# Expert tiles transposed by VectorE in 32x32 blocks, in place of four TensorE transposes per tile

## The reference, cut to what matters

```python
x = x + attention(layernorm(x), ctx, ctx)                    # 16 batches x 256 rows x 256 columns, 16 heads
x = x + moe(layernorm(x), gate_w, gate_b, w1, b1, w2, b2)    # the part that the change touches
x = x + attention2(ctx, layernorm(x), w_q, w_kv, w_out, b_out)
x = x + ffn(layernorm(x), ...)

def moe(x, gate_w, gate_b, w1, b1, w2, b2):     # 4096 rows, 8 experts, each row goes to its best 2
    logits = flat @ gate_w + gate_b
    topv, topi = lax.top_k(logits, 2)
    topw = softmax(topv)
    for each expert e:
        h = gelu(flat @ w1[e] + b1[e])          # 256 -> 1024
        out = h @ w2[e] + b2[e]                 # 1024 -> 256
        acc = acc + out * weight_of_e
```

## Time and profile before

| | |
|---|---|
| median of 3 runs | 1221.36 us |
| lowest and highest | 1218.73 and 1222.63 us |
| span of the profiled execution | 1218.4 us |
| its own time beside the span | not recorded apart; the span lies 2.96 us under the median |
| PE busy in the span | 1129.2 us, 93% |
| PEld busy | 925.1 us, 76% |
| DVE busy | 908.6 us, 75% |
| ACT busy | 743.3 us, 61% |
| POOL busy | 611.8 us, 50% |

### The profile page before, as it was taken

How to read it: one execution, slowest core, us unless ns; L and a number is a source line. 1 busy time by engine, 2 the same in 40 slices (tenths; PEclk the granted TensorE clock), 3 DMA queues, 4 the chain that set the end, 5 groups by cost and what they waited for, 6 DMA issues and landing times. The chain is left out here.

```text
span 1218.4 us, 26789 instructions
## 1 busy us (share of the span) xinstructions
PE 1129.2 (93%) x9622; PEld 925.1 (76%) x9623; DVE 908.6 (75%) x1303; ACT 743.3 (61%) x983; POOL 611.8 (50%) x607
## 2 busy tenths in 40 slices
PE   3899999989899999999999999857999999999997
PEld 2566666679788999999999999745666666668886
DVE  7899999669488888878878777567888888743332
ACT  4687778856445555554555655365877887764442
POOL 3588777344686886722002000788877876002222
PEclk9999999989899999999999999956999999999999
DMA  6577766359936465523132111165656665402221
GB/s 216 202 254 249 268 237 227 132 201 355 325 127 195 142 190 167 174 100 113 43 112 69 34 52 43 55 229 185 216 196 217 208 229 183 155 28 70 69 69 35
DMA packets 121862, 194.19 MB, mean 159 GB/s; under 512 B 12208, under 2 KB 65456, under 8 KB 121648
## 3 DMA queue, kind: packets, MB, share of 16 engines
q1 hardware_dynamic: 105520, 148.57, 35.6%
q0 software_dynamic: 12656, 39.33, 10.3%
q10 hardware_dynamic: 3600, 5.12, 1.2%
HBM read 92.85 MB, written 51.12 MB: 118 GB/s over the span
## 5 line engine op out<-in xcount | busy, mean ns | idle before, releaser
L2389 PE MATMUL y_ps<-e_w,hiddenT_hi 128*128 x624 | 225.3, 403 | 1.9 <-DVE rows L2509 1.9
L2432 ACT ACTIVATE hidden<-hidden 128x1024 f32<-128x1024 f32 x78 | 82.8, 1062 | 190.6 <-DVE hidden L2470 168.1
L2372 PE MATMUL h_ps<-kvT_hi,tile_w_hi 128*128 128x256 f32 x624 | 179.2, 287 | 6.9 <-DVE kvT_lo L2492 6.9
L1673 DVE TENSOR_REDUCE neg_max<-big 128x4 fp32r<-128x1024 f32 x128 | 154.5, 1222 | 36.4 <-PE big L1397 33.8
L2372 PE MATMUL h_ps<-kvT_lo,tile_w_hi 128*128 128x256 f32 x624 | 178.5, 286 | 0.0
L2372 PE MATMUL h_ps<-kvT_hi,tile_w_lo 128*128 128x256 f32 x624 | 178.4, 286 | 0.0
L2390 PE MATMUL y_ps<-e_w,hiddenT_lo 128*128 x624 | 175.2, 281 | 0.0
L736 DVE TENSOR_REDUCE neg_max<-big 128x4 fp32r<-128x1024 f32 x128 | 155.1, 1217 | 23.3 <-PE big L485 22.0
L1567 ACT ACTIVATE probs<-big 128x1024 f32<-128x1024 f32 x128 | 130.7, 1023 | 46.2 <-PE big L1408 44.1
L644 ACT ACTIVATE probs<-big 128x1024 f32<-128x1024 f32 x128 | 130.6, 1022 | 44.3 <-PE big L496 44.2
L2498 DVE TENSOR_TENSOR hiddenT_lo<-hidden,hiddenT_hi 128x1024 fp32r<-128x1024 f32 x78 | 98.7, 1306 | 58.2 <-ACT hiddenT_hi L2443 53.7
(11 more groups left out here) (282 smaller groups left out, 2565.8 us busy)
## 6 DMA issues: line engine op xcount, KB each, us to landing
q_stack<-q_cut SPq DMA_DIRECT2D x96, 256.0 KB, 2.6
k_stack<-k_cut SPq DMA_DIRECT2D x72, 256.0 KB, 2.7
e_w<-in_L_ffn_w POOLq DMA_DIRECT2D x10, 1024.0 KB, 6.9
slots_out<-rows SPq DMA_DIRECT2D x39, 256.0 KB
slots_in<-rows POOLq DMA_DIRECT2D x37, 256.0 KB
slot_x<-slots_in SPq DMA_DIRECT2D x37, 256.0 KB
vals<-in_v_wide SPq DMA_DIRECT2D x16, 512.0 KB, 4.4
vals<-v_wide SPq DMA_DIRECT2D x16, 512.0 KB, 4.0
```

The source lines that it names most:

```text
L1673: nc.vector.tensor_reduce(neg_max[m % 2][:, :, :, g].rearrange("p q a -> p a q").bitcast(F32R), big[bank][:], AX.X, ALU.max, negate=True). ...
L2372: last = nc.tensor.matmul(h_ps[k][:, f % HF, :], w1[w][b.u][:, c, f * P:(f + 1) * P], xT[a][b.u][:, c, :], start=(n == 0), stop=(n == 3 * ...
L2389: nc.tensor.matmul(y_ps[q][:].rearrange("p s d -> p (s d)"), hT[0][o.u][:, f, rows], both, start=(f == 0), stop=False)
L2432: nc.scalar.activation(half(hidden, k), half(hidden, k), ACT.Gelu).then_inc(gelu_done, 1)
```

## The change

The four PE transposes of a tile go, for the 37 tiles that come through `slots_in`. In their place DVE turns the tile with two `transpose` instructions, each over 128x256 elements in blocks of 32x32. Such an instruction only turns within groups of 32 partitions, so the other part of the transposition is done by the load: SP loads a tile in four DMAs (`PARTS`), each of a quarter of the columns (64) of all 256 rows, into 32 partitions. Block i of 32 rows then stands at block i of the free dimension. So that the two halves of the features (`c`) end up as the two chunks of `xT` in the right channel order, the rows in `norm2` (and so in `slots_in`) are stored with the features n and n+128 side by side (`interleaved`), and whoever reads or writes them steps over every second element.

The turned tile lies in SBUF (`turned`, the memory of `ctx_in0`), no longer in PSUM. The first two tiles are still turned by PE.

```diff
+BLOCK = 32
...
+def interleaved(row):
+    return row.rearrange("p (n c) -> p c n", c=KC)
+
+def in_order_of(row):
+    return row.rearrange("p (c n) -> p c n", c=KC)
...
-                    apply(lambda q: y_out[(b - 1) % 2][:, q, :], lambda q: norm2[(b - 1) % 2][:, q, :],
+                    apply(lambda q: in_order_of(y_out[(b - 1) % 2][:, q, :]), lambda q: interleaved(norm2[(b - 1) % 2][:, q, :]),
                           rstdb, mean_varb, rstd2_ready, norm2_ready, b - 1)
...
-                                                   norm2[f % 2][:, q, c * P:(c + 1) * P], ident[:])
+                                                   interleaved(norm2[f % 2][:, q, :])[:, c], ident[:])
...
-                    nc.vector.tensor_scalar(norm2[f % 2][:, q, :], y_out[f % 2][:, q, :], mean_varb[:, q, 0:1], rstdb[:, q:q + 1],
+                    nc.vector.tensor_scalar(interleaved(norm2[f % 2][:, q, :]), in_order_of(y_out[f % 2][:, q, :]), mean_varb[:, q, 0:1], rstdb[:, q:q + 1],
...
         def loaded(n):
-            return n.n * 16
+            return n.n * PARTS * 16
+
+        def in_parts(n, part):
+            rows = dram["slots_in"][bass.ds(n.t * SLOT_ROWS, SLOT_ROWS), part * KC * BLOCK:(part + 1) * KC * BLOCK]
+            return rows.rearrange("(i b) k -> b i k", b=BLOCK)
+
+        def of_part(n, part):
+            return x[n.u][part * BLOCK:(part + 1) * BLOCK].rearrange("b q (i k) -> b (q i) k", k=KC * BLOCK)
...
+        def transposed(n):
+            return xT_ps[:] if n.t0 < EARLY_TILES else turned
...
-                    sp.dma_start(x[n.u][:], tiled(dram["slots_in"], n.t)).then_inc(x_loaded[n.u], 16)
+                    for part in range(PARTS):
+                        sp.dma_start(of_part(n, part), in_parts(n, part)).then_inc(x_loaded[n.u], 16)
...
-                if has(n.t):
+                if has(n.t) and n.t0 < EARLY_TILES:
                     turn_x(n)
...
-                        nc.scalar.activation(xT[0][n.u][:], xT_ps[:], ACT.Copy).then_inc(xT_hi, 1)
+                        nc.scalar.activation(xT[0][n.u][:], transposed(n), ACT.Copy).then_inc(xT_hi, 1)
...
+            def turn_x(n):
+                dve.wait_ge(x_loaded[n.u], loaded(n))
+                dve.wait_ge(xT_ready, n.t)
+                alone(dve)
+                for c in range(KC):
+                    last = nc.vector.transpose(turned[:, c, :].rearrange("p (i b) -> p i b", b=BLOCK),
+                                               x[n.u][:].rearrange("p q (i a c) -> p c (q i) a", c=KC, a=BLOCK)[:, c])
+                last.then_inc(xT_filled, 1)
+
             def body(b):
                 n, o = b.shift(1), b.shift(-1)
                 if has(n.t) and n.t0 > 0:
                     places.read(n)
                     first_lo(n, 0)
+                if has(n.t) and n.t0 >= EARLY_TILES:
+                    turn_x(n)
...
-                    nc.vector.tensor_tensor(xT[1][n.u][:], xT_ps[:], xT[0][n.u][:].bitcast(F32), ALU.subtract).then_inc(xT_ready, 1)
+                    nc.vector.tensor_tensor(xT[1][n.u][:], transposed(n), xT[0][n.u][:].bitcast(F32), ALU.subtract).then_inc(xT_ready, 1)
```

More of the change, by code:

```diff
@@ L2183, in experts @@
         HF = FC // 2
-        x = first_tile["x"]
+        x, turned = first_tile["x"], first_tile["turned"]
+        PARTS = P // BLOCK
         xT = [[w[:, u, :].rearrange("p (c n) -> p c n", c=KC) for u in range(2)] for w in kvT]
@@ L2250, in body @@
                     alone(sp)
-                    sp.wait_ge(staged[n.u], loaded(n))
+                    sp.wait_ge(staged[n.u], n.n * 16)
                     alone(sp)
-                    sp.dma_start(x[n.u][:], tiled(dram["slots_in"], n.t)).then_inc(x_loaded[n.u], 16)
+                    for part in range(PARTS):
+                        sp.dma_start(of_part(n, part), in_parts(n, part)).then_inc(x_loaded[n.u], 16)
                 if has(o.t):
@@ L2348, in turn_x @@
             def turn_x(n):
-                if n.t0 < EARLY_TILES:
-                    pe.wait_ge(first_tile["gathered"][n.t0], ST * 16)
-                else:
-                    pe.wait_ge(x_loaded[n.u], loaded(n))
+                pe.wait_ge(first_tile["gathered"][n.t0], ST * 16)
                 wait(pe, xT_ready, n.t)
@@ L2356, in turn_x @@
                     for q in range(ST):
-                        last = nc.tensor.transpose(xT_ps[:, c, q * P:(q + 1) * P], x[n.u][:, q, c * P:(c + 1) * P], const["ident"][:])
+                        last = nc.tensor.transpose(xT_ps[:, c, q * P:(q + 1) * P], interleaved(x[n.u][:, q, :])[:, c], const["ident"][:])
                 last.then_inc(xT_filled, 1)
@@ L2582, in build @@
                 "x": [mb(f"slot_x{n}", [P, ST, DIM]) for n in range(EARLY_TILES)], "w1": [mb(f"tile_w1_{s}0", [P, KC, HID], F32R) for s in ("hi", "lo")],
+                "turned": ctx_own[0][:],
                 "gathered": [sem(f"tile{n}_gathered") for n in range(EARLY_TILES)], "w1_hi": sem("tile_w1_hi"), "w1_ready": sem("tile_w1_ready"),
```

## The result

The changed kernel took 1225.05 us (median of 20 runs, 1220.9 to 1235.05), the one before 1220.63 beside it (20 runs, 1216.83 to 1224.06). The ratio is 1.0048, with a 95% interval of 1.0030 to 1.0066: about half a per cent slower. The 20 times of the changed kernel fall into two groups, 13 of 1220.9 to 1225.9 us and 7 of 1230.2 to 1235.1, so the median stands at the upper edge of the lower group; the median of the 13 is 1223.56. The profiled execution has a span of 1221.4 us, against 1218.4.

A forecast was written before the change was run, and what follows sets the result against it. PE was taken to bound the kernel at 11.85 us per tile. Rounds -15.9, holds +17.9, run-up +0.8 and strided writes +0.2 make +3.0 on the 1218.4 span: 1221.4, so 1224.4 us; range 1210 to 1245.

The forecast's parts named there:

- PE's shorter round: Experts' stage: without its transposes PE's round falls from 11.85 to 11.42 us, saving 15.9 us over 37 tiles.
- The transposes on DVE, 0.8: DVE, each tile: two block transposes add 0.8 us, so its round becomes 11.46 us, level with PE's 11.42.
- The holds, +17.9: Experts' stage: POOL holds DVE 19.8 us; with the slack gone PE pays it, less the 1.9 it paid before.
- The sign that was named: Behind each POOL subtraction PE has a 2 to 5 us gap, released by `kvT_lo`; seven places, 18 us in sum.
- The run-up, +0.8: Start of the experts' stage, where tile 2 waits for DVE: one passage of the transposes' 0.8 us.
- Strided writes, +0.2: End of the first attention: the last batch's two strided writes take 0.504 us each instead of 0.410, +0.2 us.
- Late rows, costed at nothing: SP's tile loads: four DMAs in place of one leave the rows time to land, so they add 0 us.
- That leaves 4.9 us to land: Tile loads: last DMA issued at about 609.8, ACT's copy for that tile starts at 614.68, so 4.9 us remain.
- rival 3: Tile loads: 256-byte pieces land over 4.9 us after issue, each further microsecond costing up to 37 us; chance 0.05.
- Rival 1: Experts' stage, faster: PE's round stays the longer and POOL's holds cost 9.9 us less, 1211.1 us; chance 0.26.
- Rival 2: Experts' stage, slower: DVE becomes the bound if transposes exceed 0.76 us; 1231.8 at 1.0, 1245.1 at 1.36; chance 0.18.
- rival 4: First attention: PE's strided reads or POOL's strided writes come onto the path, up to 8 us, 1232; chance 0.05.

The follow-up runs named there:

- experiment 11: Changed kernel with each pair of DVE transposes done twice, the first into a spare tile: 1246.69 us, ratio 1.0217 to the kernel before.
- experiment 3: Changed kernel with each tile loaded by one DMA in pieces of 1 KB: 1220.32 us, ratio 1.0002 to the kernel before.
- experiment 9: Changed kernel with POOL's two long instructions in eight pieces each and SP loading each tile one step earlier: 1203.74 us, ratio 0.9866.
- experiment 12: Kernel before, PE still transposing, with each tile loaded by four DMAs of 64 columns: 1221.38 us, ratio 1.0014.
- experiment 4: Changed kernel with one block transpose of 128x32 in place of the two of 128x256: 1213.23 us, ratio 0.9932.

## Why the prediction was right

The forecast of 1224.4 us (span 1221.4) met 1225.05 (span 1221.4). The mechanism is shown: PE's round got shorter, DVE's came level with it, and without POOL's long instructions the loss is gone. That the spans meet exactly is luck. Two small terms were off to either side, and two were missing: the late rows, and PE's clock, which falls behind a long wait. The clock made up for PE having waited less than DVE was held. The median, too, hangs on how many runs fall into the upper group.

**PE's shorter round: right, a little too small.** Forecast 11.42 us, measured 11.36. Over 36 full rounds that is -17.5 us; the forecast's term was -15.9 for 37 tiles.

**The transposes on DVE, 0.8: they take 0.68.** Of the two ends the same-size row (0.67) was the right one; the stride of two in the read and the register load in front cost nothing that can be seen. So DVE's round is 11.30 where 11.46 was forecast. The two rounds are level as forecast (within 0.04 us then, 0.06 measured), and experiment 11 shows on which edge that is. The Trainium skill (VectorE: DVE Perf Modes, § The three transpose paths) had led to an estimate of 0.44 us for one; the trace has 0.42 for its duration, but the second starts before the first has ended, and only the 0.68 for the pair counts in a round.

**The holds, +17.9: that they are the cause is shown, their way of costing only in part.** In the stage they cost 21.66 - 5.14 = 16.5 us more than in the kernel before, from the two kernels in which POOL's instructions are short; from the third tile on, the part that the forecast's term covers, it is 20.20 - 2.45 = 17.7. But the forecast had PE pay DVE's holds one for one. From 345 us on DVE was held 20.6 us, and PE waited 13.3: four times for `kvT_lo`, 1.39, 2.10, 2.20 and 4.60 us, and at the longest round, from 401.10, 2.98 us for DVE's `rows`, which I had not foreseen. Another 7.9 us are PE's clock at its half level behind three waits, in the rounds of 14.17, 17.22 and 13.61 us (2.81, 2.88 and 2.25 us; the lines are in the last section). That the two errors cancel is luck. The sign that was named, gaps of 2 to 5 us in front of a first layer with `kvT_lo` as the releaser, seven of them and 18 us in sum, came in part: five gaps with the one of 4.51 in the run-up, 14.8 us. One subtraction made PE wait elsewhere and one not at all. The rule of the Trainium skill (SBUF — State Buffer, § Who interferes with whom), that the one that starts second waits for the whole of the first, is borne out by the experiments with pieces: an instruction of POOL an eighth as large holds DVE 0.58 us instead of 3.30.

**The run-up, +0.8: right.** Without the holds, the way from the first tile's first layer to the third's took 24.26 us in the changed kernel and 23.43 in the one before.

**Strided writes, +0.2: nothing.** DVE's strided write of `norm` takes 0.412 us where the contiguous one took 0.410, and POOL's 1.252 where it took 1.225. The rows 0.504 and 1.495 have another cause than the step of two. PE's 64 transposes for the logits, costed at nothing, do read slower with the step: a weight load takes 0.209 us where it took 0.141, and they start 0.120 us apart instead of 0.109, 0.7 us in all. The first tile starts 0.5 us later than before, which I can't put down to anything.

**Late rows, costed at nothing: wrong.** This is one of the two steps that failed. "That leaves 4.9 us to land" was worked out from PE's and ACT's undisturbed rows, and the only price for a landing was the 32% mean of the DMA engines. The mean hides when the loads collide. One place in the changed kernel, in the timelines of POOL, SP, ACT and DVE, then PE's:

```profile
634.35 0.72 POOL L1817 DMA_DIRECT2D e_w<-in_L_ffn_w  x1 [53.65 <-DVE rows L2538]
635.06 0.91 POOL L1818 DMA_DIRECT2D e_w<-in_L_ffn_w  x1
...
636.40 2.00 SPq L2275 DMA_DIRECT2D slot_x<-slots_in  x4
...
645.39 2.01 ACT L2446 ACTIVATE tile_w_hi<-e_w 128x1024 fp32r x2 [3.29 <-DMA slot_x<-slots_in]
...
646.61 5.28 DVE L2480 TENSOR_TENSOR tile_w_lo<-e_w,tile_w_hi 128x1024 fp32r<-128x1024 f32 x1 [1.74 <-ACT tile_w_hi L2446]
...
656.77 0.57 PE L2390 MATMUL h_ps<-kvT_hi,tile_w_hi 128*128 128x256 f32 x1 [4.60 <-DVE kvT_lo L2521]
```

and the busy time by stretch there (the last three columns are PE clock, DMA share and GB/s):

```profile
636.00:640.00 4.00, 4.00 (x25) 3.48 (x24) 3.71 (x4) 2.44 (x3) 0.00 (x0) 1.00 0.97 314
640.00:644.00 4.00, 4.00 (x34) 3.91 (x33) 2.82 (x4) 2.10 (x3) 0.00 (x0) 1.00 1.04 270
```

Two DMAs of 1 MB for the next expert's weights go out 2 us ahead of the tile's four quarters, all the DMA engines are busy until 644, and the rows are there at about 645.4, 9 us after the first quarter's issue. Only a few tiles meet a weight load, so it is far from the 37 us per microsecond of rival 3: in the stage it costs about 2 us, by three differences (2.2 in experiment 3, 1.8 in experiment 9, and the 1.9 below). The medians of those experiments differ by 4.7 and 6.1 us; the remainder is not placed. The Trainium skill (DMA: Bandwidth & Descriptors, § Specifications) names 512 bytes as the least for full rate. Now 51872 packets are under it, 12208 were, and with four loads in place of one ACT's waits for the rows rise from 2.3 to 13.7 us in the kernel before (experiment 12): in direction the two agree, but no run here tells the size of the pieces from their number of issues.

**PE's clock, not in the sum: missing.** This is the other step that failed: the sum took a wait of PE to cost its own length. In the changed kernel three waits were followed by the half clock, for 7.9 us in all; in the kernel before the clock was at its full level from 332.26 us to the end of the stage.

The terms of the stage as measured, in the profiled executions: -17.5 for the rounds, +0.8 for the run-up, +16.5 for the holds and the clock's falls behind them, and +1.9 that the changed kernel without holds still loses over 36 rounds of 11.36 (435.16 - 24.26 - 408.96). Together they are the +1.8 of the table, as they must be: the four are cut from the same four stages, so their sum is no test of them.

**The rivals.** Rival 1 (faster) had half its condition: the level race did go PE's way, by 0.06 us. But DVE's holds were no shorter, 20.6 us for 19.8, so its 9.9 us did not come. Rival 2 (DVE becomes the bound) was 0.08 us of transposes away by the forecast's round (0.68 against 0.76) and 0.06 by the measured one, and experiment 11 shows what lies behind. Rival 3, late rows in each tile, did not happen: only a few tiles meet them. Nor did rival 4: the first tile starts 0.5 us later, not 8.

**What stays open.** Between the changed kernel's two groups, 13 runs up to 1225.9 us and 7 from 1230.2 on, there is nothing, and the kernel before has one group. The only profile is of a run of the first group. Which holds fall where against the tiles, and how often the clock falls, may differ between them; that was not shown. Nor is it shown why PE waited 13.3 us for 20.6 us of holds.

## What to carry to other kernels

Work moved off the bounding engine can be paid twice if the other engine lands level with it: the round gets only as short as the second engine allows, and the slack is gone that used to absorb that engine's rare long delays. So before moving work, add up the rare delays of the engine that receives it (here 20 us in six places), and shorten what causes them first: cutting POOL's instruction into eight turned a loss of 4 us into a gain of 10, of which the kernel before gets 4 by the same cut. A step that is moved ahead needs its load moved ahead too: without it that edit ended 28 us behind the kernel before, with it and the pieces the kernel ended 19 us under the one before.

## What the runs showed that I had not expected

PE's clock falls behind a wait. After the wait of 4.60 us at 656.77, in the busy time by stretch of the changed kernel:

```profile
652.00:656.70 4.70, 0.17 (x2) 0.00 (x0) 4.54 (x6) 2.30 (x3) 0.20 (x1) 0.79 0.37 112
656.70:660.00 3.30, 3.23 (x15) 3.23 (x16) 1.99 (x2) 3.30 (x5) 0.00 (x0) 0.50 0.00 0
660.00:664.00 4.00, 4.00 (x29) 4.00 (x29) 3.95 (x9) 0.82 (x1) 0.00 (x0) 0.80 0.18 66
664.00:667.00 3.00, 3.00 (x21) 2.72 (x20) 3.00 (x4) 1.58 (x2) 0.00 (x0) 1.00 0.33 76
```

The clock was at the half level, 1.2 GHz, from 656.7 to some way past 660, and the round that began there took 13.61 us instead of 11.36. So a hold of 4 us on DVE cost PE the wait and 2.25 us more. Two other places in the same kernel, behind the waits of 4.51 us (to 341.49) and 2.98 us (to 410.00):

```profile
341.50:347.50 6.00, 6.00 (x28) 6.00 (x29) 4.60 (x7) 4.21 (x5) 4.78 (x6) 0.50 0.40 126
410.00:415.80 5.80, 5.80 (x18) 4.93 (x19) 5.52 (x7) 1.78 (x3) 4.75 (x5) 0.50 0.64 194
```

Behind its waits of 1.39 to 2.20 us the following rounds were 11.50 and no longer. The length of the wait alone doesn't decide it: in experiments 3 and 4 rounds of 12.89 to 13.00 us followed waits of 2.28, 2.52, 2.59 and 2.69 us, and one of 11.50 a wait of 2.53.

POOL is held by DVE as well: its eight pieces of 128x256 took 9.04 us beside DVE's work, against 5.55 for the whole in one instruction, and a piece lasts 0.73 to 0.75 us alone and up to 1.8 beside a DVE instruction with two SBUF inputs.

The block transposes are not held by POOL: eight of them ran beside its two long instructions in the changed kernel, in 0.395 to 0.439 us each, where the mean of all is 0.420.
